# A feed-forward part cut into half-token units that begin inside the layer norm, with the normalising on ScalarE

## The chip, the cores and the metric

The kernel runs on one core of a Trainium2 chip. The core has a matrix engine (TensorE, PE in the profile, with its weight loads as PEld), three engines for elementwise work (VectorE = DVE, ScalarE = ACT, GpSimd = POOL), and a queue that issues transfers (SyncE = SP). The metric is the device time of one launch in microseconds, lower is better. All matmuls write PSUM, which has eight banks of 512 f32 values per partition; most other data lies in one large SBUF buffer called `arena`, of which the tiles named below are views.

## What is computed

One sequence of 1024 tokens and 512 features goes through four residual blocks, each followed by a layer norm without weights:

```python
x = _layernorm(x + _L0_attn_ref(x, ...))   # state-space scan, 16 states
x = _layernorm(x + _L0_ffn_ref(x, ...))    # silu(x Wg^T) * (x Wu^T), then Wd^T; inner width 1792
x = _layernorm(x + _L1_attn_ref(x, ...))   # causal attention, 32 heads of 16
x = _layernorm(x + _L1_ffn_ref(x, ...))    # the same with 4-bit weights, inner width 1376

def _layernorm(x, axis=-1, eps=1e-05):
    m = jnp.mean(x, axis=axis, keepdims=True)
    v = jnp.var(x, axis=axis, keepdims=True)
    return (x - m) / jnp.sqrt(v + eps)
```

The change is in the first layer norm and the first half (gate and up) of the first feed-forward block. It also touches one small step that all four layer norms share.

## The kernel before

Each engine runs its own instructions in the order in which they are written; semaphores join them. There is no scheduler: the order in the text is the order on the engine. Tokens come in 8 tiles of 128 (`TT = 8`, `P = 128`), the inner width in 14 tiles (`M0 = 14`), and the features in 4 chunks (`DC = 4`).

**After the scan.** The residual stream lies as `xT`, features on partitions. SP issues the load of the up weights (`wu0_sb`, line 404) and of the down weights (`wd0_sb`, line 406) when the scan's last product and last sum are done, both counted on `ld_w0`.

**The first layer norm** (`norm_stage(0)` on PE, ACT, DVE). For each token tile t, PE turns the tile to token-major with four transposes (`turn_residual`, line 619) into one bank of `LN_BANKS[0]` = 4, 5, 6, 7. DVE takes its statistics (`bn_stats`, line 1306; `bn_aggr`, line 1309), adds epsilon (line 1310, into `vare`), ACT takes the root (line 969), DVE the reciprocal (line 1314), and DVE writes the normalised tile `xn` (line 1324). PE turns it back (line 596) into bank 2 or 3, ACT copies it as f16 into `xh` (line 965, "high") and DVE writes the rest, again f16, into `xl` (line 1328, "rest"). POOL keeps `xn` in `xtok` for the next residual. DVE does a tile's steps one after the other, with the statistics of tile t+1 and the rest of tile t-1 between them. PE's order is: turn tile t, turn back tile t-2, and so on.

**Gate and up** (`gate_up0`, line 650). A unit is one tile of the inner width and all 1024 tokens: 32 matmuls of 128x512 f16, 16 for the gate (2 banks) and 16 for up (2 banks): 4 chunks, each for `xh` and `xl`, each for two halves of the tokens. The first unit's first half (16 matmuls, tokens 0 to 511) stands inside the norm, ahead of the last two tiles' turning back (`between=first_gate_up0`); it waits for four tiles of `xl` and, in `gate_up0`, for banks 4 to 7 to be read out. The other 432 matmuls follow when all eight tiles are there. ACT makes `sg` = silu(gate) (line 992, 1024 columns), DVE multiplies with up (line 1362), ACT copies the product as f16 (line 994, `hh`), DVE writes the rest (line 1364, `hl`). Two units are in flight. Behind each of the first four units ACT and DVE also split one of the attention's weight matrices (lines 986 and 1355).

**Down** (`down0`, line 674). For each token tile 28 matmuls over the 14 inner tiles. It starts when all silus and all but the last rest are done.

## Time and profile before

| | us |
|---|---|
| three runs, median (lowest to highest) | 921.18 (920.85 to 922.14) |
| the profiled execution, its own time | 922.86 |
| its span in the trace | 920.9 |
| first layer norm to the first gate and up matmul | 214.85 to 232.18 |
| the other 432 gate and up matmuls | 238.37 to 331.79 |
| share of the span in which PE is busy | 91% |

Times in the trace are counted from the start of the span; 1.96 us of the launch lie outside it. PE is busy 91% of the span, DVE 71%, ACT 44%, POOL 32%. The chain of work that ended last goes through PE for 69% of the span and through DVE for 14%.

### The profile page before, as it was taken

How to read it: one execution, taken by the hardware profiler on the slowest of the kernel's cores; microseconds unless marked ns; L12 is line 12 of the kernel's file. 1: busy time of each engine (PE TensorE's matmuls, PEld its weight loads, DVE VectorE, ACT ScalarE, POOL GpSimd, SP SyncE). 2: the span in 40 equal slices, each digit the busy share in tenths (PEclk: the TensorE clock that was granted, in tenths of full speed). 3: DMA queues.
4: the chain of work that ended last, by engine and by line, in shares of the span. 5: the costliest groups of instructions: out<-in, count | busy, mean ns of one | idle time of the engine just before them, and what ended most of it. 6: DMA issues, size and time to landing. Idle time of an engine off the chain costs nothing.

```text
span 920.9 us, 19770 instructions
## 1 busy us (share of the span) xinstructions
PE 835.9 (91%) x8209; PEld 396.4 (43%) x8209; DVE 654.1 (71%) x926; ACT 408.7 (44%) x478; POOL 297.4 (32%) x211
## 2 busy tenths in 40 slices
PE   7559797986999999999988999999987999999997
PEld 2325353544444444455533344344423444444443
DVE  4998999996563334545666989999965978886334
ACT  4525666642442321253443767776665343333100
POOL 0458999993010001164420221111223222222000
PEclk8679899996999999999977999999997999999999
DMA  7800000004420000000000000000013103430011
GB/s 230 321 1 3 3 3 3 3 3 160 134 66 0 0 1 1 0 1 1 1 1 1 2 2 2 2 1 2 2 53 116 56 6 144 129 111 0 1 46 46
DMA packets 21934, 38.21 MB, mean 41 GB/s; under 512 B 6993, under 2 KB 12881, under 8 KB 21858
## 3 DMA queue, kind: packets, MB, share of 16 engines
q1 hardware_dynamic: 21858, 37.11, 11.8%
q8 instruction: 59, 0.97, 0.4%
q14 instruction: 17, 0.14, 0.0%
HBM read 34.87 MB, written 2.16 MB: 40 GB/s over the span
## 4 chain that ended last, share of the span: by engine, by line
PE 69%; DVE 14%; issue 4%; ACT 3%; POOL 2%; SPq 1%; DMA 1%; DVEq 0%; POOLq 0%; ACTq 0%
PE ps L825 12%; PE ps L650 11%; PE ps L628 8%; PE ps L852 6%; PE ps L776 6%; DVE arena L1393 6%; PE ps L674 5%; PE ps L712 5%; PE ps L760 3%; POOL arena L1103 2%; PE ps L493 2%; DVE arena L1248 2%; PE ps L543 2%; PE ps L689 2%; PE ps L716 2%
## 5 line engine op out<-in xcount | busy, mean ns | idle before, releaser
L1393 DVE TENSOR_REDUCE arena<-ps 128x1 f32<-128x512 f32 (+3 forms) x320 | 183.6, 629 | 22.9 <-PE ps L716 15.9
L1050 ACT ACTIVATE arena<-ps 128x1024 f32<-128x1024 f32 (+2 forms) x160 | 144.2, 941 | 81.8 <-PE ps L760 81.6
L1103 POOL TENSOR_TENSOR arena<-arena 128x1024 f32<-128x1024 f32 x64 | 156.9, 2485 | 54.2 <-DVE arena L1248 52.6
L1248 DVE TENSOR_TENSOR_SCAN arena<-arena,ps 128x1024 f32<-128x1024 f32 x64 | 142.4, 2271 | 8.9 <-PE ps L543 6.7
L825 PE MATMUL ps<-arena 128*128 128x512 f16 x528 | 114.3, 379 | 1.6 <-DVE arena L1328 1.6
L1150 POOL TENSOR_SCALAR_AFFINE_SELECT arena<-arena 128x512 f32<-128x512 f32 x64 | 42.6, 667 | 189.4 <-ACT arena L1050 189.4
L712 PE MATMUL ps<-arena 64*128 64x512 f16 (+3 forms) x384 | 98.1, 344 | 1.0 <-DVE arena L1393 1.0
L944 ACT ACTIVATE arena<-arena,negA 128x1024 f32<-128x1024 f32 x64 | 72.6, 1147 | 58.9 <-DVE arena L1248 57.1
L650 PE MATMUL ps<-arena 128*128 128x512 f16 x448 | 97.2, 379 | 1.6 <-DVE arena L1328 1.6
L543 PE MATMUL ps<-arena 64*128 64x64 f16 x3072 | 61.2, 197 | 35.6 <-DVE arena L1248 28.5
L543 PEld LDWEIGHTS ps<-arena 64*128 64x128 f16 x3072 | 53.4, 99 | 86.1 <-DVE arena L1248 67.3
L628 PE MATMUL ps<-arena 128*128 128x512 f16 x384 | 86.9, 379 | 3.1 <-DVE arena L1328 1.6
L776 PE MATMUL ps<-arena 128*32 128x512 f32 (+3 forms) x768 | 84.8, 515 | 1.9 <-POOL arena L1150 1.9
L760 PE MATMUL ps<-arena 64*128 64x512 f16 (+3 forms) x384 | 77.9, 342 | 6.0 <-DMA arena<-arena 4.3
L825 PEld LDWEIGHTS ps<-arena 128*128 128x128 f16 x528 | 51.6, 98 | 63.6 <-DVE arena L1328 1.8
L493 PE MATMUL ps<-arena,ident_sb 64*64 64x512 f32 x512 | 73.9, 653 | 3.7 <-POOL arena L1103 3.6
L650 PEld LDWEIGHTS ps<-arena 128*128 (+1 forms) x448 | 43.9, 98 | 54.3 <-DVE arena L1328 1.8
L712 PEld LDWEIGHTS ps<-arena 64*128 64x128 f16 x384 | 29.3, 94 | 82.7 <-DVE arena L1393 70.1
L852 PE MATMUL ps<-arena 128*128 128x512 f16 x264 | 57.1, 379 | 0.0
L628 PEld LDWEIGHTS ps<-arena 128*128 128x128 f16 x384 | 36.3, 98 | 45.2 <-DVE arena L1302 1.9
L716 PE MATMUL ps<-mask_b,picks_b 64*128 64x128 bf16 x512 | 52.8, 221 | 0.0
L674 PE MATMUL ps<-arena 128*128 128x512 f16 x224 | 49.3, 379 | 0.0
(145 smaller groups left out, 976.7 us busy)
## 6 DMA issues: line engine op xcount, KB each, us to landing
arena<-in_w_q_dram SPq DMA_DIRECT2D x11, 768.0 KB, 4.2
arena<-c_rows SPq DMA_DIRECT2D x16, 512.0 KB, 10.9
arena<-in_w_s_dram SPq DMA_DIRECT2D x11, 384.0 KB, 4.6
arena<-in_x_fm_dram SPq DMA_DIRECT2D x8, 256.0 KB, 3.9
out_dram<-arena SPq DMA_DIRECT2D x8, 256.0 KB, 2.0
arena<-in_wg_dram SPq DMA_DIRECT2D x1, 1792.0 KB, 9.8
arena<-in_wu_dram SPq DMA_DIRECT2D x1, 1792.0 KB, 7.2
arena<-in_wd_dram SPq DMA_DIRECT2D x1, 1792.0 KB, 10.7
```

The lines of the kernel that those rows point to most:

```text
L543: last = nc.tensor.matmul(ps[:, 2 * (i % 2) + r, q * SUB:(q + 1) * SUB], dtx_tok[c % 2][rows, s, q, :], diag[n][rows, e, q, :], start=(k = ...
L628: last = nc.tensor.matmul(banks(bank, 1), part[:, c, ds(t * P, P)], wsp[:, w, s, c, :], start=(c == 0 and part is src_h and s == 0), stop= ...
L650: last = nc.tensor.matmul(banks(bank + h, 1), w[:, c, ds(m * P, P)], part[:, c, h * HALF:(h + 1) * HALF], start=(c == 0 and part is xh), s ...
L712: last = nc.tensor.matmul(dst, q_st[rows, 2 * g + r, i * P:(i + 1) * P], k_st[rows, 2 * g + r, key:key + w], start=True, stop=not diag)
L760: last = nc.tensor.matmul(ps[:, 3 + 2 * (e % 2) + b, at * (hi - lo):(at + 1) * (hi - lo)], k_st[rows, 2 * g + r, j * P:(j + 1) * P], q_st[ ...
L776: last = nc.tensor.matmul(ps[32 * a:32 * a + 32, 7, lo - HALF * half:HALF], v_ring[g % 2][:, j, a, :], p_t[n % 4][:, a, 0:hi - lo], start= ...
L825: last = nc.tensor.matmul(banks(bank + h, 1), gu[u][:, s, w * DC + c, :], part[:, c, h * HALF:(h + 1) * HALF], start=(c == 0 and s == 0 an ...
L852: last = nc.tensor.matmul(banks(u, 1), part[:, m, ds(t * P, P)], wd1[:, s, m, :], start=(m == 0 and part is h1h and s == 0), stop=(m == M1 ...
L1050: nc.scalar.activation(dst, src, ACT.Exp, scale=float(HD) ** -0.5).then_inc(exp_done, 1)
L1103: nc.gpsimd.tensor_tensor(hC[i % 4][:], hst[i % 3][:], c_all[:, n, :], ALU.mult).then_inc(hc_done, 1)
L1248: nc.vector.tensor_tensor_scan(hst[i % 3][:], dA[i % 3][:], banks(2 * (i % 2), 2), 0.0, ALU.mult, ALU.add).then_inc(scan_done, 1)
L1393: nc.vector.reduce_max(maxima_slot(half, k), ps[:, ring_bank(n), 0:len(heads) * w].rearrange("p (a w) -> p a w", a=len(heads)), AX).then_i ...
```

## The change

1. **Units.** A unit is now one inner tile and half the tokens: 16 matmuls, 8 for the gate in one bank and 8 for up in another. There are 28: the 14 tiles for tokens 0 to 511, then the 14 for tokens 512 to 1023. Up to four units are in flight (only two among the first four and the last four), so `sg` and `h32` have four slots of 512 columns. The loops are written out.
2. **Start.** PE turns the residual of tiles 0 to 3, turns back tiles 0 to 3 with tiles 4 and 5 of the residual between them, and then begins unit 0. The residual of tiles 6 and 7 and the turning back of tiles 4 to 7 stand between units 0 to 3. `LN_BANKS[0]` is now 0, 1, 4, 5, 0, 1, 0, 1.
3. **Normalising on ACT.** In the first norm, ACT writes `xn` as rstd * x + shift straight from PSUM; DVE makes `shift` = -mean * rstd, 128x1. The rest of DVE's steps stay.
4. **Epsilon.** In all four norms the root takes epsilon as its bias (`eps_sb`); DVE's addition into `vare` is gone. One small memset is added at the start of the program.
5. **Around it.** The down weights have their own semaphore `ld_wd0`, waited for at the first down matmul. The first four token tiles of down wait for the first 14 units' rests (and for 24 products, which frees banks 0 and 1), the later ones for all 28. The attention's weights are split behind units 6 to 9, each wait of theirs with them.

```diff
-LN_BANKS = ((4, 5, 6, 7), (0, 1), (0, 1), (0, 1))
+LN_BANKS = ((0, 1, 4, 5, 0, 1, 0, 1), (0, 1), (0, 1), (0, 1))
...
-        sg = view(104, 2 * T, f32).rearrange("p (b t) -> p b t", b=2)
-        h32 = view(112, 2 * T, f32).rearrange("p (b t) -> p b t", b=2)
+        sg = view(104, 4 * HALF, f32).rearrange("p (b t) -> p b t", b=4)
+        h32 = view(112, 4 * HALF, f32).rearrange("p (b t) -> p b t", b=4)
...
-        vare = small("vare", [P, 2])
+        eps_sb = small("eps_sb", [P, 1])
         sdev = small("sdev", [P, 2])
-        rstd = small("rstd", [P, 1])
+        rstd = small("rstd", [P, 2])
+        shift = small("shift", [P, 2])
...
+        UNITS0 = 2 * M0
+        def unit0_slot(n):
+            return n % 4 if 4 <= n < UNITS0 - 4 else n % 2
+        def unit0_before(n):
+            return next((o for o in range(n - 1, -1, -1) if unit0_slot(o) == unit0_slot(n)), None)
+        def unit_banks(slot):
+            return ((6, 7), (4, 5), (2, 3), (0, 1))[slot]
...
-            sp.dma_start(wd0_sb[:], wd0.rearrange("(m p) d -> p m d", p=P)).then_inc(ld_w0, 16)
+            sp.dma_start(wd0_sb[:], wd0.rearrange("(m p) d -> p m d", p=P)).then_inc(ld_wd0, 16)
...
-            def gate_up0(m, u, halves=(0, 1), first=False):
-                for w, bank, free, signal in ((wg0_sb, 4 - 4 * u, silu_done, gate_done), (wu0_sb, 6 - 4 * u, h_done, up_done)):
-                    if not first:
-                        pe.wait_ge(free, m - 1)
-                    elif halves == (0,):
-                        pe.wait_ge(x_normed, bank + 1)
+            def gate_up0(n):
+                h, m = divmod(n, M0)
+                gate, up = unit_banks(unit0_slot(n))
+                before = unit0_before(n)
+                for w, bank, free, signal in ((wg0_sb, gate, silu_done, gate_done), (wu0_sb, up, h_done, up_done)):
+                    if before is not None:
+                        pe.wait_ge(free, before + 1)
                     for c in range(DC):
                         for part in (xh, xl):
-                            for h in halves:
-                                last = nc.tensor.matmul(banks(bank + h, 1), w[:, c, ds(m * P, P)],
-                                                        part[:, c, h * HALF:(h + 1) * HALF],
-                                                        start=(c == 0 and part is xh), stop=(c == DC - 1 and part is xl))
-                    if halves != (0,):
-                        last.then_inc(signal, 1)
-            def first_gate_up0():
-                pe.wait_ge(ld_w0, 3 * 16)
-                pe.wait_ge(xl_done, TT // 2)
-                gate_up0(0, 0, (0,), first=True)
-            norm_stage(0, turn_residual, straight=True, between=first_gate_up0)
-            pe.wait_ge(xl_done, TT)
-            gate_up0(0, 0, (1,), first=True)
-            gate_up0(1, 1, first=True)
-            with pe.Fori(1, M0 // 2) as k:
-                for u in range(2):
-                    gate_up0(2 * k + u, u)
+                            last = nc.tensor.matmul(banks(bank, 1), w[:, c, m * P:(m + 1) * P], part[:, c, h * HALF:(h + 1) * HALF],
+                                                    start=(c == 0 and part is xh), stop=(c == DC - 1 and part is xl))
+                    last.then_inc(signal, 1)
+            def turn_first(t):
+                if t >= 4:
+                    pe.wait_ge(x_normed, (1, 2, 5, 6)[t - 4])
+                turn_residual(t, LN_BANKS[0][t]).then_inc(ln_in, 1)
+            def turn_normed(t):
+                pe.wait_ge(x_normed, t + 1)
+                if t >= 2:
+                    pe.wait_ge(xl_done, t - 1)
+                for c in range(DC):
+                    last = nc.tensor.transpose(ps[:, 2 + t % 2, c * P:(c + 1) * P], xn[:, t % 2, c * P:(c + 1) * P], ident_sb[:])
+                last.then_inc(x_turned, 1)
+            for t in range(4):
+                turn_first(t)
+            turn_normed(0)
+            turn_normed(1)
+            turn_first(4)
+            turn_normed(2)
+            turn_first(5)
+            turn_normed(3)
+            pe.wait_ge(ld_w0, 2 * 16)
+            pe.wait_ge(xl_done, TT // 2)
+            gate_up0(0)
+            turn_first(6)
+            turn_normed(4)
+            gate_up0(1)
+            turn_first(7)
+            turn_normed(5)
+            gate_up0(2)
+            turn_normed(6)
+            gate_up0(3)
+            turn_normed(7)
+            for n in range(4, UNITS0):
+                if n == 6:
+                    pe.wait_ge(xl_done, TT)
+                gate_up0(n)
             def down0(t, u):
                 for m in range(M0):
-                    if isinstance(t, int) and t == 0 and m == M0 - 1:
+                    if isinstance(t, int) and t == 0 and m == 0:
+                        pe.wait_ge(ld_wd0, 16)
                         pe.wait_ge(hl_done, M0)
+                        pe.wait_ge(h_done, UNITS0 - 4)
+                    if not (isinstance(t, int) and t < TT // 2) and m == 0:
+                        pe.wait_ge(hl_done, UNITS0)
                     for part in (hh, hl):
                         last = nc.tensor.matmul(banks(u, 1), part[:, m, ds(t * P, P)], wd0_sb[:, m, :],
                                                 start=(m == 0 and part is hh), stop=(m == M0 - 1 and part is hl))
                 return last
-            pe.wait_ge(silu_done, M0)
-            pe.wait_ge(hl_done, M0 - 1)
             norm_stage(1, down0, between=first_projections)
...
                 def root(t, u):
                     act.wait_ge(var_done, TT * ln + t + 1)
-                    nc.scalar.activation(sdev[:, u:u + 1], vare[:, u:u + 1], ACT.Sqrt).then_inc(sdev_done, 1)
+                    nc.scalar.activation(sdev[:, u:u + 1], mv[:, u, 1:2], ACT.Sqrt, bias=eps_sb[:]).then_inc(sdev_done, 1)
...
+            def first_normalise(t):
+                u = t % 2
+                act.wait_ge(shift_made, t + 1)
+                if t >= 2:
+                    act.wait_ge(x_kept, t - 1)
+                    act.wait_ge(x_turned, t - 1)
+                nc.scalar.activation(xn[:, u, :], banks(LN_BANKS[0][t], 1), ACT.Identity, bias=shift[:, u:u + 1],
+                                     scale=rstd[:, u:u + 1]).then_inc(x_normed, 1)
...
+            def gate_taken(n):
+                act.wait_ge(gate_done, n + 1)
+                if n >= 4:
+                    act.wait_ge(h_done, n - 3)
+                nc.scalar.activation(sg[:, n % 4, :], banks(unit_banks(unit0_slot(n))[0], 1), ACT.Silu).then_inc(silu_done, 1)
+            def product_high(n):
+                h, m = divmod(n, M0)
+                act.wait_ge(h_done, n + 1)
+                nc.scalar.copy(hh[:, m, h * HALF:(h + 1) * HALF], h32[:, n % 4, :]).then_inc(hh_done, 1)
+            first_root(0)
+            first_root(1)
+            first_normalise(0)
+            first_root(2)
+            first_normalise(1)
+            first_high(0)
+            first_root(3)
+            first_normalise(2)
+            first_high(1)
+            first_normalise(3)
+            first_high(2)
+            first_root(4)
+            first_high(3)
+            first_normalise(4)
+            first_root(5)
+            first_normalise(5)
+            for n in range(UNITS0):
+                gate_taken(n)
+                if n < 2:
+                    first_root(6 + n)
+                    first_normalise(6 + n)
+                if n < 4:
+                    first_high(4 + n)
+                product_high(n)
+                if 6 <= n < 10:
+                    weight_high(n - 6)
...
                 def variance(t, u):
-                    own.done(nc.vector.bn_aggr(mv[:, u, :], st6[:]))
-                    nc.vector.tensor_scalar(vare[:, u:u + 1], mv[:, u, 1:2], EPS, None, ALU.add).then_inc(var_done, 1)
+                    nc.vector.bn_aggr(mv[:, u, :], st6[:]).then_inc(var_done, 1)
+                    dve.wait_ge(var_done, TT * ln + t + 1)
                 def root_taken(t, u):
                     dve.wait_ge(sdev_done, TT * ln + t + 1)
-                    own.done(nc.vector.reciprocal(rstd[:], sdev[:, u:u + 1]))
+                    own.done(nc.vector.reciprocal(rstd[:, 0:1], sdev[:, u:u + 1]))
...
+            def first_stats(t):
+                dve.wait_ge(ln_in, t + 1)
+                own.done(nc.vector.bn_stats(st6[:], banks(LN_BANKS[0][t], 1)))
+                if t >= 2:
+                    dve.wait_ge(sdev_done, t - 1)
+                nc.vector.bn_aggr(mv[:, t % 2, :], st6[:]).then_inc(var_done, 1)
+                dve.wait_ge(var_done, t + 1)
+            def first_shift(t):
+                u = t % 2
+                dve.wait_ge(sdev_done, t + 1)
+                if t >= 2:
+                    dve.wait_ge(x_normed, t - 1)
+                own.done(nc.vector.reciprocal(rstd[:, u:u + 1], sdev[:, u:u + 1]))
+                nc.vector.scalar_tensor_tensor(shift[:, u:u + 1], mv[:, u, 0:1], -1.0, rstd[:, u:u + 1], ALU.mult, ALU.mult).then_inc(shift_made, 1)
+            def first_rest(t):
+                dve.wait_ge(xh_done, t + 1)
+                nc.vector.tensor_tensor(xl[:, :, t * P:(t + 1) * P], ps[:, 2 + t % 2, :].rearrange("p (c t) -> p c t", c=DC),
+                                        xh[:, :, t * P:(t + 1) * P], ALU.subtract).then_inc(xl_done, 1)
...
+            def product(n):
+                dve.wait_ge(silu_done, n + 1)
+                dve.wait_ge(up_done, n + 1)
+                if n >= 4:
+                    dve.wait_ge(hl_done, n - 3)
+                nc.vector.tensor_tensor(h32[:, n % 4, :], sg[:, n % 4, :], banks(unit_banks(unit0_slot(n))[1], 1), ALU.mult).then_inc(h_done, 1)
+            def product_rest(n):
+                h, m = divmod(n, M0)
+                dve.wait_ge(hh_done, n + 1)
+                at = slice(h * HALF, (h + 1) * HALF)
+                nc.vector.tensor_tensor(hl[:, m, at], h32[:, n % 4, :], hh[:, m, at], ALU.subtract).then_inc(hl_done, 1)
...
+            first_stats(0)
+            first_stats(1)
+            first_shift(0)
+            first_stats(2)
+            first_shift(1)
+            first_stats(3)
+            first_shift(2)
+            first_rest(0)
+            first_shift(3)
+            first_rest(1)
+            first_stats(4)
+            first_rest(2)
+            first_rest(3)
+            first_shift(4)
+            first_stats(5)
+            first_shift(5)
+            for n in range(UNITS0):
+                product(n)
+                if n < 2:
+                    first_stats(6 + n)
+                    first_shift(6 + n)
+                if n < 4:
+                    first_rest(4 + n)
+                product_rest(n)
+                if 6 <= n < 10:
+                    weight_low(n - 6)
...
```

On PE, from the end of the scan, the order before is this (L619 turns the residual, L596 turns back, L650 is gate and up):

```order
L619 MATMUL ps<-ident_sb,arena 128x128 x12
L596 MATMUL ps<-ident_sb,arena 128x128 x4
L619 MATMUL ps<-ident_sb,arena 128x128 x4
L596 MATMUL ps<-ident_sb,arena 128x128 x4
L619 MATMUL ps<-ident_sb,arena 128x128 x4
L596 MATMUL ps<-ident_sb,arena 128x128 x4
L619 MATMUL ps<-ident_sb,arena 128x128 x4
L596 MATMUL ps<-ident_sb,arena 128x128 x4
L619 MATMUL ps<-ident_sb,arena 128x128 x4
L596 MATMUL ps<-ident_sb,arena 128x128 x4
L619 MATMUL ps<-ident_sb,arena 128x128 x4
L596 MATMUL ps<-ident_sb,arena 128x128 x4
```

Then come 16 matmuls of L650, 8 of L596, and the rest of L650. After the change PE has, from the first turning back on (L632 turns the residual, L678 turns back, L664 is gate and up):

```order
L678 MATMUL ps<-ident_sb,arena 128x128 x8
L632 MATMUL ps<-ident_sb,arena 128x128 x4
L678 MATMUL ps<-ident_sb,arena 128x128 x4
L632 MATMUL ps<-ident_sb,arena 128x128 x4
L678 MATMUL ps<-ident_sb,arena 128x128 x4
L664 MATMUL ps<-arena 128x512 x16
L632 MATMUL ps<-ident_sb,arena 128x128 x4
L678 MATMUL ps<-ident_sb,arena 128x128 x4
L664 MATMUL ps<-arena 128x512 x16
L632 MATMUL ps<-ident_sb,arena 128x128 x4
L678 MATMUL ps<-ident_sb,arena 128x128 x4
L664 MATMUL ps<-arena 128x512 x16
```

The first 16 matmuls of gate and up have moved from behind the turning of all eight residual tiles and six of the tiles back to behind six and four; six groups of transposes that stood ahead of or beside them now stand between units.

On ACT, from the end of the norm's first part, the order after the change is this (L1023 root, L1031 normalising, L1036 high, L1047 silu, L1052 copy of the product); before, all roots and highs were done ahead of the first silu, with one table load between them:

```order
L1031 ACTIVATE arena<-ps,shift,rstd 128x512
L1047 ACT_TABLE_LOAD
L1047 ACTIVATE arena<-ps 128x512
L1023 ACT_TABLE_LOAD
L1023 ACTIVATE sdev<-mv,eps_sb 128x1
L1031 ACTIVATE arena<-ps,shift,rstd 128x512
L1036 CAST arena<-ps 128x4x128
L1052 CAST arena<-arena 128x512
L1047 ACT_TABLE_LOAD
L1047 ACTIVATE arena<-ps 128x512
L1023 ACT_TABLE_LOAD
```

The roots of tiles 6 and 7 have moved in between the silus of units 0, 1 and 2, and each change from the one function to the other and back loads a table: five loads up to the silu of unit 2 where there was one.

## Rows read from the trace of the kernel before

**Rows 1.** Windows: PE, PEld, DVE, ACT, POOL busy (instructions), granted clock, DMA.
```profile
214.85:232.50 17.65, 12.64 (x57) 10.38 (x58) 15.80 (x40) 5.08 (x13) 3.69 (x6) 0.60 0.58 183
232.50:238.40 5.90, 4.34 (x25) 2.34 (x24) 3.95 (x9) 2.72 (x5) 1.23 (x2) 1.00 0.91 346
238.40:331.80 93.40, 93.40 (x433) 42.35 (x434) 40.97 (x30) 35.10 (x32) 3.75 (x2) 1.00 0.10 27
```

**Rows 2.** The chain that ended last around the first norm: start, length, what.
```profile
215.98 0.71 DVE st L1306
...
231.27 1.11 PE ps L596 x4
232.38 3.55 PE ps L650 x16
...
236.41 0.59 ACT arena L965
237.03 1.30 DVE arena L1328 x2
```

**Rows 3.** The same chain further on, its long pieces.
```profile
238.37 93.41 PE ps L650 x432
331.79 18.13 PE ps L674 x84
...
728.26 0.44 PE ps L596 x4
728.70 2.59 PE ps L628 x12
```

**Rows 4.** Timeline of one token tile in the first norm: start, length, engine, line.
```profile
226.64 0.69 DVE L1306 BATCH_NORM_STATS2 st<-ps 128x6 f32<-128x512 f32 x1
...
227.36 0.16 DVE L1314 RECIPROCAL rstd<-sdev 128x1 f32<-128x1 f32 x1
227.43 0.59 ACT L965 CAST arena<-ps 128x512 f32 x1 [1.80 <-PE ps L596]
227.56 0.18 DVE L1309 BATCH_NORM_AGGREGATE mv<-st 128x2 f32<-128x6 f32 x1
227.78 0.15 DVE L1310 TENSOR_SCALAR vare<-mv 128x1 f32<-128x1 f32 x1
227.86 0.81 DVE L1324 TENSOR_SCALAR arena<-ps,mv,rstd 128x512 f32<-128x512 f32 x1
227.96 0.20 ACT L969 ACTIVATE sdev<-vare 128x1 f32<-128x1 f32 x1
228.59 0.68 DVE L1328 TENSOR_TENSOR arena<-ps,arena 128x512 f16<-128x512 f32 x1
```

**Rows 5.** Timeline of ACT near the start, without and with a 128x1 operand.
```profile
18.70 0.70 ACT L880 ACTIVATE arena<-arena,series_sb 128x512 f16<-128x512 f32 x1
19.32 0.61 ACT L881 ACTIVATE arena<-arena 128x512 f32<-128x512 f32 x1
```

**Rows 6.** Timeline of ACT between the last root and the first silu.
```profile
237.50 1.28 ACT L992 ACT_TABLE_LOAD   x1
```

**Rows 7.** Windows of the norm, columns as in rows 1, for the granted clock.
```profile
212.00:222.00 10.00, 6.99 (x33) 5.00 (x26) 7.13 (x17) 3.53 (x7) 1.23 (x2) 0.50 0.96 323
222.50:225.50 3.00, 1.25 (x10) 0.86 (x8) 2.86 (x9) 1.21 (x4) 0.62 (x1) 1.00 0.31 97
226.00:232.00 6.00, 4.67 (x20) 3.87 (x21) 5.79 (x15) 1.48 (x4) 1.85 (x3) 0.50 0.18 7
```

**Rows 8.** Timeline of PE's transposes at the higher clock, and of SP's load.
```profile
211.57 0.38 SPq L404 DMA_DIRECT2D arena<-in_wu_dram  x1
...
223.64 0.65 PE L596 MATMUL ps<-ident_sb,arena 128*128 128x128 f32 x4 [0.98 <-DVE arena L1324]
```

**Rows 9.** The page's DMA issues: KB each, us from issue to landing.
```profile
arena<-in_wu_dram SPq DMA_DIRECT2D x1, 1792.0 KB, 7.2
```

48 lines of the change are left out of this document (13 added, 35 removed).

## The prediction

> **What bounds the kernel now.** I read the windows by stage first, then the chain of waits, then the timeline of one tile. The windows show three stretches around the change [rows 1]. In the first, 214.85 to 232.5 us, DVE is busy for 15.80 of 17.65 us, while PE has only transposes: the first layer norm is bound by DVE. In the third, 238.4 to 331.8 us, PE is busy all the time at the full granted clock: gate and up are bound by PE. The second is the seam: 16 gate and up matmuls are run early, and then PE stands for 1.5 us at the end of the norm. The chain of waits says the same [rows 2]. It goes from the first statistics at 215.98 through DVE, tile by tile, up to the transposes at 231.27, the 16 early matmuls at 232.38, the copy and the two rests at 236.41 and 237.03, and then without a break through 432 matmuls [rows 3]. These take 93.41 us, 0.2162 us each, so all 448 need 96.9 us of PE. They cover 214.85 to 331.79, 116.9 us. So 20.0 us of PE's time around the norm hold no gate and up work. This is what the change can win from. A token tile costs DVE 0.69 + 0.16 + 0.18 + 0.15 + 0.81 + 0.68 us, 2.67, and with small overlaps about 2.55; the rest of tile 3, the last of these rows, ends at 229.27 [rows 4].
>
> **Part 1, normalising on ACT.** DVE loses the 0.81 us and the addition of 0.15, and gains `shift`, a 128x1 step that I price like the addition, 0.15 [rows 4]. That leaves DVE 1.9 us a tile. ACT gains the normalising. No row shows it. An ACT instruction on 128x512 out of PSUM takes 0.59 [rows 4], and a 128x1 operand adds about 0.1 (0.70 against 0.61) [rows 5]. The new one has two such operands, so I take 0.82, with bounds 0.59 (they cost nothing beyond) and 0.94. By the same row the root with its bias goes from 0.20 to 0.30. ACT then has 0.30 + 0.82 + 0.59 = 1.7 us a tile and was idle most of the time there (5.08 of 17.65 busy) [rows 1].
>
> **Part 2, when unit 0 can begin.** I walk the engines' new orders by hand with these durations and 0.04 us for each hand-over. The first statistics stay at 215.98. The first normalising starts at 218.2; tiles 0 to 3 are normed by 219.0, 220.3, 222.0 and 223.4. ACT is the tight engine here: from 218.2 it has four normalisings, four highs and three roots, 6.5 us, and with its short waits ends the fourth high at 225.1. DVE then writes the fourth rest by 225.8, where it was 229.3 before. Unit 0 begins at 225.9 instead of the 232.2 of the 16 early matmuls. The weights are no obstacle: the up weights are issued at 211.57 [rows 8] and take 7.2 us to landing [rows 9], so they are there by 218.8; the down weights, issued behind them, are now waited for only at the first down matmul, 100 us later.
>
> **Part 3, from there PE's queue alone.** Behind 225.9 PE has 448 matmuls, 96.9 us, and six groups of four transposes, 0.44 us each at the full clock [rows 3]: 2.6 us. That would end gate and up at 325.4. That one unit writes eight matmuls in a row into one bank adds nothing: in the attention's projections twelve in a row into one bank take 2.59 us, 0.216 each [rows 3]. The copies of weights behind units 6 to 9 keep their cost; each unit leaves ACT and DVE about 2 us free, and with up to four units in flight the walk shows no wait of PE.
>
> **Part 4, the loop through the tables.** The new order puts the roots of tiles 6 and 7 between the silus, and only two units may be in flight until unit 4. From silu 0 to silu 1, and again to silu 2, ACT has: silu 0.59, load of the root's table 1.28, a wait of 0.3 for the statistics, root 0.30, 0.4 for DVE's reciprocal and shift, normalising 0.82, high 0.59, product's copy 0.59, load of the silu's table 1.28. That is 6.2 us a round [rows 4, 6]. Silu 0 can start at 229.8 (the table is loaded by then), so silu 2 ends at 242.9. PE reaches unit 4, which needs that silu's bank, 16.5 us after 225.9, at 242.4. PE so waits 0.5 us; the cover is used up, and every further microsecond on this loop would be paid in full. The end of gate and up goes to 325.9.
>
> Here a rule of the Trainium skill speaks against the change. The row shows that a table load takes 1.28 us [rows 6]. The page "ScalarE: Activation LUTs", section "Table sets: the hidden batching unit", says to batch calls by set and not by function, and gives about 2.7 us for a load. By the page's figure the walk ends gate and up at about 332.4 us, no better than now; the trace's duration is used, so the sum keeps 325.9.
>
> **Part 5, the clock.** PE's granted clock was at the lower of its two levels, 1.2 GHz, in 212 to 222, with transposes for 6.99 of 10 us. It was at 2.4 GHz in 222.5 to 225.5, where PE was busy for only 1.25 of 3 us; it then fell again, and stayed low from 226 to 232 with 4.67 of 6 us busy [rows 7]. From 232.5 on it is full [rows 1]. In my walk PE has three groups of transposes between 222 and 225.9 and waits for the rest of it, as sparse as the stretch before the fall. So I expect the first matmuls at the lower level. The bounds are none of it, and the whole low stretch with PE at work nearby, which by these rows is 6 to 7 us long; I take the middle, 3.4 us, which costs half of that, 1.7 us. It gives ACT time, so the 0.5 us of part 4 vanishes. Sum: 325.4 + 1.7 = 327.1, against 331.79: **4.7 us** sooner.
>
> **Part 6, what follows.** Down starts with its first four token tiles, which need units 0 to 13 alone, and banks 0 and 1, free after unit 23; both are past by then, so PE runs on as it does at 331.79 now [rows 3]. The later tiles need the last rest, which comes about 2.5 us after the last unit, against 24 us of down. The addition of epsilon is gone in 24 more tiles, but in the second norm PE sets the pace (28 matmuls a tile), and in the third too: 0.44 + 2.59 = 3.03 us is the whole period of a tile [rows 3]. Only the starts and the end of the norms are on the path, 0.04 to 0.07 each, less than what the bias adds to the root. I take -0.1, with bounds -0.3 and +0.3. The memset at the start lies beside the loads. Written-out loops add no work; one row of 432 matmuls shows no gap for the loop that there was, so nothing is gained either.
>
> **The sum.** -4.7 - 0.1 = -4.8 us. The profiled execution took 922.86 us, 1.68 more than the median of the three runs; on its own scale the forecast is 918.1. Taken to the median, 921.18 - 4.8 = **916.4 us**.
>
> **Rivals.**
> 1. *Full clock from the start.* The transposes now come more densely, and the clock stays up. End of gate and up 325.9, so 915.2; with a normalising of 0.59 us the walk gives 325.0 and 914.2. For it: the loss of part 5 is read from one fall only. Against: that fall came after just such a sparse stretch.
> 2. *The four tiles come no sooner.* If ACT's chain in the norm is as long as DVE's was (tile 3 ready at 229.3), then only PE's order gains: 229.3 + 96.9 + 2.6 = 328.8, -3.0, and up to 1.7 of clock on top: 918.2 to 919.9, about 918.8. Against: the tile's work is now split 1.9 to 1.7 between two engines, where 2.55 stood on one.
> 3. *The table loop binds* (no change). It decides when a round costs ACT more than 6 us; at 7.5 us a round, by longer loads, or waits where I have hand-overs, unit 4 comes about 3 to 5 us later and the time is 919.5 to 921.5, about 920.5. For it: slack is nil. Against: the row of 1.28.
> 4. *Slower: low clock through the mixed stretch.* The clock counts on a busy PE; if waits of units 1 to 4 on the table loop keep it at 1.2 GHz, 64 matmuls and 24 transposes take 33 us instead of 16.5. That costs 16.5 against the 6.4 us of room: 921.18 + 10 = 931. It decides at 12.8 us of low clock. Against: PE has long, unbroken stretches of 3.5 us there, and the rise by 232.5 came after less.
>
> **How the numbers follow.** The forecast has 0.62, rival 1 0.15, rival 2 0.12, rival 3 0.07, rival 4 0.04. The forecast's own bounds: clock 0 to 3.4, stall 0 to 1, normalising, later norms; 914.7 to 918.5. The range takes in rivals 1 and 2, 914.0 to 919.2, and leaves out rivals 3 and 4. About 0.2% (1.8 us) can be told from no change. Faster by more than that: the forecast, rivals 1 and most of 2, 0.88; within it: rest of 2 and rival 3, 0.08; slower 0.04.
>
> **What would show it.** The first gate and up matmul near 225.9 (rival 2: 229.3). A few matmuls of 0.43 us pitch, then 0.216. The last one at about 327.1, and no idle PE before the first down matmul. Normalising near 0.8 us on ACT. Five table loads of 1.28 before the silu of unit 2, and a wait of PE ahead of unit 4 of 0 to 0.5 us (rival 3: several). The forecast would be wrong if the fourth rest came after 227, if PE waited for silus in more than one place, or if another stage, above all the attention, changed its length.

## The result: 913.8 us, 7.1 us faster, 2.3 us more than forecast

| | before | changed |
|---|---|---|
| median of the runs measured side by side (lowest to highest), us | 920.85 (918.77 to 922.14) | 913.77 (911.17 to 915.73) |
| ratio, with its 95% interval | | 0.9921 [0.9903, 0.9939] |
| the profiled execution, its own time and its span, us | 922.86, 920.9 | 914.36, 912.6 |
| from the first transpose of the norm to the last gate and up matmul ("the seam"), us | 116.5 | 110.7 |
| attention: first key product to first gate and up product of the last block, us | 263.5 | 258.9 |

The forecast was 916.4 us with a range of 914.0 to 919.2. The time is just below the range, and the sign is right. The changed kernel measured again gave 0.9906 [0.9887, 0.9925] and 913.72 us.

The windows by stage are those of [rows 1] and [rows 7] (columns as there: PE, PEld, DVE, ACT, POOL busy, granted clock, DMA):

```profile
212.00:222.00 10.00, 6.40 (x35) 4.27 (x36) 4.82 (x12) 4.11 (x7) 2.86 (x3) 0.71 0.64 220
222.00:226.50 4.50, 3.99 (x20) 3.55 (x19) 3.87 (x11) 3.97 (x7) 1.97 (x4) 0.50 1.03 325
226.50:228.59 2.09, 0.59 (x7) 0.39 (x6) 1.62 (x5) 0.88 (x2) 0.05 (x1) 1.00 0.00 0
228.59:245.10 16.51, 16.51 (x88) 8.95 (x88) 7.43 (x19) 14.18 (x20) 2.47 (x4) 1.00 0.39 128
245.10:327.90 82.80, 82.78 (x385) 37.50 (x385) 43.89 (x56) 37.51 (x57) 3.75 (x2) 1.00 0.11 31
```

Between 228.59 and 245.10, where units and tiles are mixed, PE is busy all the time and ACT for 14.18 of 16.51 us. The hole of 1.5 us behind the early matmuls, seen in the second window of [rows 1], is gone. One of 1.5 us now stands ahead of unit 0, where PE waits for the high copy and the rest of tile 3 (227.13 and 227.75 in the chain below). The chain that ended last shows the same, and is to be read against [rows 2] and [rows 3] (L1433 statistics, L1031 normalising, L632 and L678 transposes, L1036 high, L1449 rest, L664 gate and up, L715 down):

```profile
218.30 0.71 DVE st L1433
...
222.22 0.79 ACT arena L1031
...
223.05 1.12 PE ps L678 x4
224.16 0.85 PE ps L632 x4
225.02 0.85 PE ps L678 x4
225.87 0.79 PE ps L632 x4
226.66 0.45 PE ps L678 x4
...
227.13 0.60 ACT arena L1036
...
227.75 0.70 DVE arena L1449
...
228.59 3.61 PE ps L664 x16
232.20 0.44 PE ps L632 x4
232.64 0.44 PE ps L678 x4
233.07 3.45 PE ps L664 x16
...
251.84 76.41 PE ps L664 x354
328.25 11.87 PE ps L715 x55
```

This execution lost 2.3 us before the norm: its first statistics are at 218.30, where [rows 2] have 215.98. In it the input projection's last matmul starts at 17.0 us, in the kernel before at 14.0; in the other profile of the changed kernel it is 14.2. So the stage is measured from its own start. Difference of the spans, 8.3 us: start -2.3 (a loss), seam +5.8, attention +4.6, the rest 0.2. For the pair of profiles taken later (c1 and c2 below, 918.5 and 911.2): start -0.9, seam +6.2, attention +1.9, the rest 0.1. In these two pairs the seam is steady. The attention differs as well, by an amount that varies, though the change touches in it nothing but epsilon.

The down weights' own semaphore did no work in these profiles: in the changed kernel both loads have landed before unit 0 starts (up 221.85, down 227.01, unit 0 228.59; in its second profile down 224.02, unit 0 226.89).

### The profile page after: what moved, and what is told of

Same layout as the page of the kernel before. It is cut to its first block, busy times and chain, and to the rows that moved or that the text cites. A ratio compares the mean times of both kernels' runs of the same rounds, so it can differ in the third digit from the quotient of the medians.

```text
span 912.6 us, 19633 instructions
## 1 busy us (share of the span) xinstructions
PE 831.6 (91%) x8209; PEld 394.4 (43%) x8209; DVE 650.5 (71%) x923; ACT 427.2 (47%) x518; POOL 297.2 (33%) x211
## 4 chain that ended last, share of the span: by engine, by line
PE 68%; DVE 13%; issue 4%; ACT 3%; POOL 3%; DMA 1%; SPq 1%; POOLq 0%; DVEq 0%; ACTq 0%
PE ps L864 13%; PE ps L664 11%; PE ps L641 8%; PE ps L891 6%; DVE arena L1518 6%; PE ps L815 5%; PE ps L715 5%; PE ps L751 4%; PE ps L799 3%; POOL arena L1182 3%; PE ps L506 2%; DVE arena L1328 2%; PE ps L556 2%; PE ps L728 2%; PE ps L755 1%
## 5 line engine op out<-in xcount | busy, mean ns | idle before, releaser
L664 PE MATMUL ps<-arena 128*128 128x512 f16 x448 | 97.5, 379 | 1.5 <-DVE arena L1449 1.5
L864 PEld LDWEIGHTS ps<-arena 128*128 128x128 f16 x528 | 51.6, 98 | 63.6 <-DVE arena L1408 1.8
L664 PEld LDWEIGHTS ps<-arena 128*128 128x128 f16 x448 | 43.7, 98 | 53.7 <-issue 1.7
L641 PEld LDWEIGHTS ps<-arena 128*128 128x128 f16 x384 | 36.4, 98 | 45.0 <-DVE arena L1382 1.8
L715 PE MATMUL ps<-arena 128*128 128x512 f16 x224 | 49.3, 379 | 0.0
## 6 DMA issues: line engine op xcount, KB each, us to landing
arena<-in_wd_dram SPq DMA_DIRECT2D x1, 1792.0 KB, 11.4
```

The lines of the kernel that those rows point to most:

```text
L641: last = nc.tensor.matmul(banks(bank, 1), part[:, c, ds(t * P, P)], wsp[:, w, s, c, :], start=(c == 0 and part is src_h and s == 0), stop= ...
L664: last = nc.tensor.matmul(banks(bank, 1), w[:, c, m * P:(m + 1) * P], part[:, c, h * HALF:(h + 1) * HALF], start=(c == 0 and part is xh), ...
L864: last = nc.tensor.matmul(banks(bank + h, 1), gu[u][:, s, w * DC + c, :], part[:, c, h * HALF:(h + 1) * HALF], start=(c == 0 and s == 0 an ...
```

## Experiments

In each table row "seam" and "attention" are as above. "first unit" is the time from the norm's first transpose to the first gate and up matmul; "matmuls" is from there to the last one's start. Ratio and median come from 4 to 12 executions of each kernel. The other four columns come from one profiled execution each, and are differences of times read to 0.1 us, so they can be off by 0.1.

| | ratio to before | median us | first unit | matmuls | seam | attention |
|---|---|---|---|---|---|---|
| before | | 920.85 | 17.3 | 99.2 | 116.5 | 263.5 |
| c1 before, again | 0.9996 [0.9982, 1.0009] | 920.92 | 16.6 | 100.5 | 117.1 | 261.2 |
| changed | 0.9921 [0.9903, 0.9939] | 913.77 | 11.4 | 99.3 | 110.7 | 258.9 |
| c2 changed, again | 0.9906 [0.9887, 0.9925] | 913.72 | 11.7 | 99.2 | 110.9 | 259.3 |
| e1 epsilon only | 0.9989 [0.9974, 1.0004] | 919.95 | 16.9 | 99.6 | 116.5 | 259.8 |
| e2 ACT normalises, old order | 1.0038 [1.0024, 1.0053] | 924.84 | 19.7 | 100.1 | 119.8 | 261.1 |
| e3 the same, ACT's queue reordered | 1.0017 [0.9997, 1.0037] | 923.49 | 17.1 | 100.6 | 117.7 | 261.2 |
| e4 new order, DVE normalises | 0.9948 [0.9933, 0.9964] | 916.89 | 12.8 | 101.2 | 114.0 | 259.1 |
| e5 new units, no early start | 1.001 [0.9998, 1.0021] | 923.15 | 20.6 | 99.3 | 119.9 | 259.1 |
| e6 changed, addition of epsilon back | 0.9915 [0.9903, 0.9928] | 913.91 | 11.4 | 100.8 | 112.2 | 258.1 |
| e7 before, 58 more PE instructions | 1.0002 [0.9986, 1.0017] | 920.32 | 16.4 | 99.4 | 115.8 | 261.1 |
| e8 changed, 82 more | 0.9892 [0.9874, 0.9909] | 911.66 | 11.5 | 99.3 | 110.8 | 257.3 |
| e9 changed, table loads doubled | 0.9996 [0.9984, 1.0008] | 920.41 | 11.7 | 106.1 | 117.8 | 259.6 |
| e10 before, 116 more | 0.9973 [0.9962, 0.9985] | 918.92 | 17.2 | 100.5 | 117.7 | 261.3 |
| e11 changed, 123 more | 0.9894 [0.9879, 0.9908] | 912.75 | 11.2 | 99.2 | 110.4 | 256.2 |
| e12 changed, 166 more | 0.9917 [0.9899, 0.9935] | 914.17 | 11.4 | 100.8 | 112.2 | 260.7 |
| e13 before, 207 more | 0.9983 [0.9971, 0.9995] | 919.90 | 17.3 | 100.8 | 118.1 | 257.6 |

**The two kernels again** (c1, c2), for how much one profile tells.

> The kernel before, unchanged, as a control. Theory A (the change acts only between the first transposes of the norm and the last gate and up matmul; the other differences between the two profiles are scatter of single executions): ratio 1.000 +- 0.002, but stretches outside the seam move between profiles of the same kernel by as much as they did between before and after: the start up to the last x_proj matmul (14.0 us before, 17.0 after) and the first attention steps (477.1 to 499.8 before, 473.6 to 494.0 after) by 2 to 4 us. Theory B (the change itself shortens the attention by 3.9 us): the attention stretch repeats within 0.5 us of the first profile of before.

> The changed kernel, unchanged. Theory A: ratio near 0.993, first norm transpose to last gate and up matmul again 110.7 us (before 116.5), if the granted clock is again full when unit 0 begins; 112.4 if it is at the lower level for 3.4 us. The attention stretch 473.6 to 692.9 (219.3 us; before 223.1) changes by 2 us or more. Theory B: it stays within 0.5 us of 219.3.

The seam repeats within 0.6 us. The attention of the kernel before does not: it differs by 2.3 us between two executions of one kernel, that of the changed kernel by 0.4. One profile of each kernel therefore tells little of the attention.

### The parts of the change

**e1, epsilon alone.** The kernel before, with this in all four norms:

```diff
-                    nc.scalar.activation(sdev[:, u:u + 1], vare[:, u:u + 1], ACT.Sqrt).then_inc(sdev_done, 1)
+                    nc.scalar.activation(sdev[:, u:u + 1], mv[:, u, 1:2], ACT.Sqrt, bias=eps_sb[:]).then_inc(sdev_done, 1)
```

> The kernel before with epsilon as the root's bias in all four norms, nothing else. My forecast had -0.1 us (bounds -0.3 to +0.3) for the three later norms. In the first norm DVE loses one 128x1 step a tile that mostly overlapped (0.08 each): -0.6 us. Together -0.7, ratio 0.9992. Rival: epsilon carries more of the gain, since what lies behind the seam moved by 2.4 us in the profiles (3.5 ahead after gate and up, 8.2 at the end, less 3.0 late at the start): -2 us or more, ratio 0.998 or less.

0.9989, with 1 inside the interval; the seam is unchanged at 116.5. **e6** asks the same from the other side: the changed kernel with DVE's addition in the last three norms.

```diff
-                    nc.vector.bn_aggr(mv[:, u, :], st6[:]).then_inc(var_done, 1)
-                    dve.wait_ge(var_done, TT * ln + t + 1)
+                    own.done(nc.vector.bn_aggr(mv[:, u, :], st6[:]))
+                    nc.vector.tensor_scalar(vare[:, u:u + 1], mv[:, u, 1:2], EPS, None, ALU.add).then_inc(var_done, 1)
```

> The changed kernel with the addition of epsilon on VectorE restored in norms two to four. By my walk +0.1 to +0.3 us. The changed kernel gains 7.1 to 7.8 us in all, and only 5.8 to 6.0 of it lie in the seam. Theory A (the rest is scatter): ratio to before as that of the changed kernel, 0.990 to 0.993. Rival (epsilon makes the rest): +1.5 us, ratio 0.993 to 0.994, and the stretches behind the seam that differ would come back.

0.9915 against 0.9921 and 0.9906: epsilon is worth nothing that can be told, and the attention's gain is not epsilon's (e6 does without that part of the change and has 258.1).

**e2 and e3, the normalising alone.** e1, and in the first norm ACT normalises; PE's order and the units are those of before. In e2 ACT's queue has a tile's copy `high` behind the next tile's normalising:

```diff
+                    for t in range(2, TT):
+                        root(t, t % 2)
+                        act_norm(t - 1, (t - 1) % 2)
+                        high(t - 2, t % 2)
```

> The kernel before with epsilon as bias and the first norm's normalising on ScalarE, but with the old order on PE and the old units of 1024 tokens. Eight tiles by 1.9 us of DVE instead of 2.55: the last rest comes some 4 to 5 us sooner, if PE's old order does not bind; PE's 16 early matmuls then start at about 228 instead of 232. My theory: -3.5 to -4.5 us against before, that is the larger part of the gain is the split of the tile between the two engines. Rival: ACT's chain binds as DVE's did (rival 2 of the prediction): -1 us or less.

It is slower by 0.4%, where 3.5 to 4.5 us less were expected. The chain of e2, one tile's round (L1373 and L1376 statistics, L1385 shift, L976 normalising, L966 high):

```profile
222.21 0.70 DVE st L1373
...
222.93 0.19 DVE mv L1376
...
223.34 0.17 DVE shift L1385
...
223.54 0.78 ACT arena L976
...
224.32 0.48 ACT arena L966
...
225.43 0.70 DVE st L1373
```

DVE waits for `high` before its rest, `high` stands behind the normalising, that waits for DVE's shift, and the next statistics stand behind the rest: 3.2 us a tile, where DVE alone took 2.55 [rows 4]. In e3 `high` stands ahead of the normalising:

```diff
-                        act_norm(t - 1, (t - 1) % 2)
                         high(t - 2, t % 2)
+                        act_norm(t - 1, (t - 1) % 2)
```

> As the run with the old PE order and old units and the normalising on ScalarE, but on ScalarE each tile's high copy stands ahead of the next tile's normalising, where that run had it behind. In its trace the steps stats, shift, normalising, high, rest of neighbouring tiles formed one serial loop of 3.2 us a tile (before: 2.55). Theory A (that loop was an artefact of my order): now DVE binds at 1.9 us a tile, first transposes to last gate and up matmul 112 to 114 us (before 116.5), time -3 to -4.5 us. Rival (moving the normalising to ScalarE costs more in hand-overs than it relieves DVE, whatever the order): 116 us or more, no gain.

2.47 us a tile, by the spacing of the statistics in its chain, and the time of before (1.0017, with 1 inside the interval); 1.9 us a tile had been expected. So moving 0.81 us from the bounding engine to a mostly idle one gained nothing by itself: the tile's steps still went through both engines one after the other.

**e4, the order alone.** The changed kernel, with DVE normalising in one step again; ACT's normalising is left out:

```diff
-                nc.vector.scalar_tensor_tensor(shift[:, u:u + 1], mv[:, u, 0:1], -1.0, rstd[:, u:u + 1], ALU.mult, ALU.mult).then_inc(shift_made, 1)
...
+                nc.vector.tensor_scalar(xn[:, u, :], banks(LN_BANKS[0][t], 1), mv[:, u, 0:1], rstd[:, u:u + 1],
+                                        ALU.subtract, ALU.mult).then_inc(x_normed, 1)
```

> The changed kernel with the first norm's normalising back on VectorE, order and units as changed. DVE then has, up to the fourth rest, five statistics of 0.9, four reciprocals of 0.2, four normalisings of 0.81 and four rests of 0.69: 11.3 us from the first statistics, so unit 0 begins 12.4 us after the first transpose (changed kernel 11.4 to 11.7). Theory A (the early start carries the gain): 1 us slower than the changed kernel, ratio to before 0.992 to 0.994. Rival (the split of the tile carries it): 3 us slower or more, ratio 0.995 or above.

The first unit comes 1.1 to 1.4 us later than with ACT, and the seam is 114.0: 3.2 us longer than in the changed kernel, still 2.5 to 3 shorter than before. The other 2 us are clock in this profile. Two windows of e4:

```profile
222.00:228.20 6.20, 3.50 (x17) 2.73 (x15) 5.47 (x12) 2.23 (x5) 1.36 (x3) 0.51 0.45 141
228.20:236.00 7.80, 7.75 (x31) 3.69 (x32) 4.11 (x9) 3.91 (x6) 1.23 (x2) 0.73 0.01 2
```

The transposes ran at the lower level to the end and the first matmuls began there. That DVE's normalising brought this lower level is not shown: e6 and e12 below pay 1.6 us of the same kind with ACT normalising. By the ratios e4 (0.9948) is 2.5 to 3.9 us slower than the changed kernel (0.9921, 0.9906); its interval overlaps that of the first result and lies clear of those of c2 and e6. So the early start carries more than half of the gain. The two recorded theories had 0.992 to 0.994 and 0.995 or above, and the result stands between them.

**e5, the units without the early start.** The changed kernel; all eight tiles are normed first (the same lines move ahead in ACT's and DVE's queues, so no table is exchanged between the first units):

```diff
-            pe.wait_ge(xl_done, TT // 2)
-            gate_up0(0)
...
             turn_normed(7)
-            for n in range(4, UNITS0):
+            pe.wait_ge(xl_done, TT)
+            for n in range(UNITS0):
```

> The changed kernel, but unit 0 begins only when all eight tiles are normed; no table swap in between. Eight tiles at 1.9 us from the first statistics end about 16.5 us after the first transpose, then 96.9 us without a break: 113.5 us to the last matmul, against 110.7 with the early start and 116.5 before. Time 2.8 us above the changed kernel. Rival: the interleaving costs as much as it gains (swaps, clock), then within 1 us of the changed kernel.

The first unit starts 20.6 us after the first transpose, where 16.5 were expected, and the gain is gone (1.001). Part of this is my order of the last tiles, in which tiles 5 to 7 again went through ACT and DVE one at a time. Another part is the clock: the granted clock is 0.50 from 236.02 to 241.60, the first 5.6 us of matmuls, and by the table the matmuls then take 99.3 us where 447 times 0.216 are 96.6: a cost of some 2.7 us, by this estimate. So the seam of 119.9 is longer than it need be, and what the units gain without the early start is not measured cleanly. What e5 does show is that this kernel without its early start gains nothing; and that, with the seam lost, its attention was still at 259.1.

### The loop through the tables

**e9.** The changed kernel, and in each of the two rounds a silu and a root of one column on ACT, which bring two more table loads:

```diff
                     first_root(6 + n)
+                    nc.scalar.activation(spare[:, 2 * n:2 * n + 1], eps_sb[:], ACT.Silu)
+                    nc.scalar.activation(spare[:, 2 * n + 1:2 * n + 2], eps_sb[:], ACT.Sqrt)
                     first_normalise(6 + n)
```

> The changed kernel with two more table loads and two 1-column activations in each of the two rounds between silu 0 and silu 2 (the root's and the silu's table alternately). My walk had the loop at 6.2 us a round and no slack: the end of gate and up would come 2 x 2.7 = 5.2 us later, first transposes to last gate and up matmul 116 us, time 5 us above the changed kernel. Rival (the loop has slack, since PE's own work up to unit 4 is as long): 1 to 3 us. If the price of a load were the page's 2.7 us and not 1.28, twice that.

Two groups of lines from the timelines: first the changed kernel's second round (ACT, and PE's unit 4), then e9's second round.

```profile
238.49 0.60 ACT L1047 ACTIVATE arena<-ps 128x512 f32<-128x512 f32 x1
239.11 1.28 ACT L1023 ACT_TABLE_LOAD   x1
...
240.67 0.30 ACT L1023 ACTIVATE sdev<-mv,eps_sb 128x1 f32<-128x1 f32 x1 [0.28 <-DVE mv L1436]
...
241.45 0.78 ACT L1031 ACTIVATE arena<-ps,shift,rstd 128x512 f32<-128x512 f32 x1 [0.48 <-DVE shift L1445]
...
243.25 1.28 ACT L1047 ACT_TABLE_LOAD   x1
...
244.54 0.60 ACT L1047 ACTIVATE arena<-ps 128x512 f32<-128x512 f32 x1
...
245.20 1.04 PE L664 MATMUL ps<-arena 128*128 128x512 f16 x4
```

```profile
239.30 1.28 ACT L1024 ACT_TABLE_LOAD   x1
...
241.18 1.28 ACT L1075 ACT_TABLE_LOAD   x1
...
242.68 1.28 ACT L1076 ACT_TABLE_LOAD   x1
...
245.86 1.28 ACT L1048 ACT_TABLE_LOAD   x1
246.19 1.09 PE L679 MATMUL ps<-ident_sb,arena 128*128 128x128 f32 x4 [3.22 <-DVE arena L1452]
247.15 0.60 ACT L1048 ACTIVATE arena<-ps 128x512 f32<-128x512 f32 x1
...
247.80 4.58 PE L665 MATMUL ps<-arena 128*128 128x512 f16 x11 [0.52 <-ACT arena L1048]
```

In the changed kernel a round takes 6.05 us from silu to silu; the third silu ends at 245.14, and unit 4, which needs its bank, starts at 245.20. It is exactly in time. In e9 a round takes 8.46 us, 2.41 more, for two loads of 1.28 and two small steps of 0.20, less a wait for DVE of 0.48 that they cover and small overlaps. PE stands 3.2 and 0.5 us; its transposes then take 1.09 us, where the same view has 0.60 elsewhere, which is the lower clock level, and the 11 matmuls 0.42 each. The two rounds are 4.8 us longer and the seam 6.9, so the whole gain of the kernel is lost. What the loop gains in length is paid in full, and the clock on top.

### What the attention gave

Without added waits (all but e7, e8 and e10 to e13), the kernels with the new units had an attention of 258.1 to 259.6 us, those with the old ones 259.8 to 263.5. A place in the chain where they differ is the last of its 16 groups of four small row transfers. First the kernel before (c1 reads the same, 2.41 at the end), then c2, the changed kernel again:

```profile
683.25 0.59 SPq L426
683.88 2.49 DMA arena<-arena
```

```profile
676.23 0.59 SPq L439
...
676.87 1.70 DMA arena<-arena
```

The view of transfers in the 4 us around this group (682 to 686) shows for the kernel before one more packet, which is not data:

```profile
q8 instruction: 1, 0.02, 1.6%
arena<-arena SPq DMA_DIRECT2D x4, 1.0 KB, 2.3
```

and for c2 none in 3.6 us, with

```profile
arena<-arena SPq DMA_DIRECT2D x4, 1.0 KB, 1.7
```

Such a packet brings 16 KB of instructions. By their places they are PE's: in the attention they come about every 250 records of PE and PEld. So their place depends on the length of PE's program ahead of them. The written-out loops changed that length. In all 17 profiles, each group of row transfers that took 3.7 us or more from its first issue to its last landing, where others take 3.5 to 3.6, had such a packet within that time; not each group with a packet was late.

The experiments add redundant waits of PE late in the scan, where all it waits for is long there; two of them share one instruction, and an odd one has one of its own. For e7, the kernel before:

```diff
+                    if 31 <= i < 60:
+                        for _ in range(4):
+                            pe.wait_ge(warm_set, 1)
```

> The kernel before with 116 redundant waits added on TensorE (four ahead of each of 29 steps at the end of the scan, on a semaphore that has long its value); nothing else. In the five profiles with the old units a 16384-byte instruction packet lies over two of the attention's small row transfers, which then land in 2.2 to 3.1 us; in the five with the new, written-out units it lies elsewhere and they land in 1.6 to 1.7. Theory L (layout: TensorE's longer program shifts the places where its instructions are fetched): the pads shift them as the new units do, the second and the last group of row transfers land in 1.7, keys first to last 219.5 us instead of 221, and the time is 1.5 to 2.5 us below before, less what the waits cost in the scan (0 to 1.5). Rival: the transfers are slower for another reason; landing stays at 2.2 to 3.1, no gain.

> The changed kernel with 140 redundant waits on TensorE (five ahead of each of 28 steps at the end of the scan). Theory L: with 116 places of the shift taken up to a full 256, the instruction packet lies over the two groups of row transfers again: landing 2.2 to 3.1 us, keys first to last about 221, the time 1.5 to 2.5 us above the changed kernel, ratio to before about 0.994, plus what the waits cost (0 to 1.8). Rival: landings stay at 1.7, the time moves only by the waits.

e7's 116 waits became only 58 instructions (19828 instructions in the profile, 19770 before), so the packet moved half as far as meant, still within the last group, and the time stayed. e8 (140 waits, 82 instructions) was expected to be slower than the changed kernel. It moved other groups into and out of reach and has the lowest median of the study, 911.66 us, with an interval that overlaps that of the changed kernel. e10 (8 waits in place of 4) and e11 (9 in each of 25 steps) followed:

> The kernel before, computing all, with 232 redundant waits of TensorE in the late steps of the scan. The 116 waits of the last such run became 58 instructions, two waits to one, so these should be 116 more instructions, about what the changed kernel has more of (its instruction packet lies 129 records further from the end). Theory (place of TensorE's instruction packets against the small row transfers of the attention): the last and the second of the sixteen groups of row transfers, which took 4.1 to 4.8 us to land in the kernel before, take 3.5 as in the changed kernel; the attention from its first key product to its last matmul gets 1.0 to 2.5 us shorter (before 223.1 and 220.5 us), less what the extra waits cost in the scan (under 0.5 us), median 919 to 920.5 against 921. Rival (the attention's gain has another cause in the changed kernel, such as the state of its queues or of the clock): the pattern of the groups may move, the attention keeps 220.5 to 223 us and the time is the same or 0.3 us more.

> The changed kernel, computing all, with 225 redundant waits of TensorE in the late steps of the scan, some 125 instructions more: with the 129 that it already has it comes to about 256, one whole instruction packet, so the packets should lie against the row transfers as in the kernel before. Theory (place of the packets): the second, fourth and last groups of row transfers take 4.1 to 4.8 us again, the attention takes 220.5 to 223 us instead of 219.3 to 219.8, and the time is 915 to 916.3 instead of 913.75, so that the gain left is that of the seam, 5 to 6 us. Rival (another cause): attention and time as in the changed kernel, 913.5 to 914.2.

In e10 the packet left the last group; its chain there ends with

```profile
683.69 0.59 SPq L426
684.33 1.69 DMA arena<-arena
```

and its 160 exponentials keep c2's distance from the first one within 0.1 us up to the 32nd and 0.8 us to the end. The time is 2.5 us better than before (0.9973), by redundant instructions alone. Its profile, a slow one for its kernel (921.63 us, median 918.92), does not show that gain in the attention, 261.3 us: it avoids c1's 2.3 us in the last group, but loses 2.4 us that c1 does not lose, 1.2 of them in the first groups. e11, expected at 915 to 916.3 us, went past the place I aimed at: the packets were still some 20 to 50 records from those of the kernel before, no group from the tenth on was late, the attention was the shortest of all, 256.2 us, and the median 912.75. So I aimed twice more, e12 (11 waits in each of 28 steps) at the place of before in the changed kernel, e13 (15 in each of 26) at e11's place in the kernel before:

> The changed kernel, computing all, with 308 redundant waits of TensorE in the late steps of the scan, two to an instruction: 168 more instructions. With 125 more (the run before this one) its instruction packets still lay 31 to 54 records from those of the kernel before, and no group of row transfers from the tenth to the sixteenth waited for one; 168 should bring them to within some 10 records of the kernel before. Theory (place of the packets): the second, fourth, seventh to ninth, fourteenth and last groups take 4.1 us and more as in the kernel before and the thirteenth 3.5; the attention from its first key product to the first gate or up product of the second feed-forward part takes 260.5 to 263 us (before 261.2 and 263.5, changed kernel 258.9 and 259.3, with 125 more 256.2); the ratio to the kernel before is 0.992 to 0.996, 2 to 4 us above the kernel with 125 more (0.9894). Rival (the written-out units help the attention in another way): attention 256 to 259.5 us, ratio 0.989 to 0.992.

> The kernel before, computing all, with 390 redundant waits of TensorE in the late steps of the scan, two to an instruction: 208 more instructions. That should bring its instruction packets to where they lay in the changed kernel with 125 more. Theory: the groups of row transfers from the tenth on take 3.5 us, the attention takes 256 to 258.5 us instead of 261.2 and 263.5, the scan may pay up to 1 us for the waits; ratio 0.994 to 0.997. Rival (only the written-out units gain there): attention 260 to 262 us, ratio 0.9995 to 1.002.

The last group in e12's chain, then in e13's:

```profile
677.47 1.63 SPq L439
679.14 0.59 SPq L439
679.77 1.70 DMA arena<-arena
```

```profile
682.92 0.59 SPq L426
683.55 1.70 DMA arena<-arena
```

The row transfers came out near what was aimed at in e12, less so in e13, where the eleventh and the fourteenth group are late (4.1 us each). In e12 one issue takes 1.63 us, the second, fourth, seventh, eighth, fourteenth and last groups are late again (and the twelfth, which was not late before; the ninth is on time), and the attention takes 260.7. In e13 it takes 257.6, 3.6 less than c1. Yet in the times little of this arrives: e12 with 0.9917 is between the two results of the changed kernel, and e13 with 0.9983 gained 1.6 us. In e13's profile 3.6 us were lost ahead of the attention (first transpose at 215.6 for c1's 214.3, seam 118.1, and from the seam to the attention 146.9 instead of 145.6 us), so that its span is c1's, 918.5.

What follows. **Shown** is that a packet beside a group of row transfers makes them late, and that redundant PE instructions alone can lower the time of the kernel before: 0.9973 [0.9962, 0.9985] in e10, against 1.0002 [0.9986, 1.0017] in e7. In the changed kernel the same kind of edit gave 0.9892 to 0.9917, which is not clear of noise (e8, e11 and e12 have intervals that overlap). Within one kernel the attention moved by 3.7 to 4.5 us with the added instructions (257.6 to 261.3 before, 256.2 to 260.7 changed), more than the 2.3 us between two profiles of one and the same kernel, but each of these is one profile.

**Not shown** is that this is why the changed kernel's attention is shorter. With like places it remains shorter, e12 against c1 by 0.5 us, c2 against e10 by 2.0, e11 against e13 by 1.4; all three are below those 2.3 us. Over four places each, the mean ratio is 0.9904 for the changed kernel (0.9914, 0.9892, 0.9894, 0.9917) and 0.9989 for the one before (0.9996, 1.0002, 0.9973, 0.9983): 7.8 us apart, of which the seam is 6. The cause of the last 1 to 2 us stays open.

One thing goes along with the attention's length over the 17 profiles, and that is how long the granted clock was at the lower level in it: 31.8 us of the 263.5 before, 29.8 of 261.2 in c1, 23.1 of 259.3 in c2, 22.5 of 258.9 in the changed kernel's first profile, 18.5 of 257.6 in e13 and 17.4 of 256.2 in e11. Over the 17 a microsecond more at the lower level goes with 0.43 us more of attention. Before, c1, e2, e3 and e7 have a spell of it that begins 206 to 209 us after the first key product, right behind the late last group; none of the kernels in which that group is on time has one there. The late transfers may so cost more through the clock than by their own delay. Which is cause and which effect these runs do not tell, and e1 and e12 have a late last group without the spell.

## The prediction, point by point

**What bounds it: right.** The 20 us around the norm without gate and up work were where most of the gain was; 448 matmuls and six groups of transposes from 228.59 to 328.25 take 99.7 us, forecast 96.9 + 2.6.

**Part 1, right.** The normalising took 0.78 us for 0.82, the root 0.30 as forecast. `shift` took 0.16 us at most tiles, but 0.55 to 0.58 at two where it ran beside other work. What the prediction did not see is that part 1 brings nothing without part 2 (e2, e3); with it, it is worth 1.1 to 1.4 us of the start, and 2.5 to 3.9 us in all by e4's ratio.

**Part 2, right in kind.** Unit 0 was forecast 9.9 us behind the first statistics and came 10.3 behind (228.59 - 218.30). Rival 2, the four tiles no sooner, is out.

**Part 3, right.** 3.45 us for 16 matmuls (0.216 each), 0.44 for a group of transposes.

**Part 4, right to some tenths of a microsecond.** Before the silu of unit 2 there were five loads of 1.28 us; a round took 6.05 us for 6.2, with no slack and no stall. "Every further microsecond on this loop would be paid in full" is what e9 shows, 6.9 us for 4.8. Rival 3 lies one table load away. The Trainium skill's page "ScalarE: Activation LUTs", section "Table sets: the hidden batching unit", gives about 2.7 us a load, by which the gain was nil; the rows of 1.28 decided, and e9 shows what longer loads would have done. Its advice to batch by set is to be weighed by slack: four extra loads cost nothing here, eight cost all.

**Part 5, the step that failed in the seam: the 1.7 us.** It was to come from the lower clock in the first 3.4 us of matmuls. In the changed kernel's two profiles it was 0: in the second window above, the transposes run at 0.50 with PE busy 3.99 of 4.50 us, and the clock rises at 226.5, ahead of unit 0. I had expected it high at 222 with a sparse PE behind it. The low clock made the transposes slow enough to stand back to back (chain above, 223.05 to 226.66), where PE in [rows 7] had pauses. That they do so does not decide it alone: in e12 the same five groups stand back to back at the lower level, from 220.61 to 225.1, and the clock rose only at 230.1. (The Trainium skill's page "TensorE: Matmul & The Clock Gate", section "Part 4: PE-mode transpose", says that transposes do not count as a busy TensorE in the same way. Here the clock rose at 226.5 with nothing but f32 transposes on PE since 217.17, so for these the trace does not bear it out.) But the price was not wrong, only its chance. In e12 (and e6 alike) the clock was high before 219.8 and fell for the transposes; e12's window and its first matmuls:

```profile
226.60:234.00 7.40, 7.37 (x31) 3.54 (x32) 2.79 (x9) 5.30 (x7) 1.23 (x2) 0.77 0.01 2
```

```profile
226.63 5.30 PE ps L667 x16
```

5.30 us for 16 matmuls instead of 3.61 is 1.7 us, the number forecast, and e12 and e6 have seams of 112.2. Of the six profiles whose first norm and loop are those of the change (changed, c2, e6, e8, e11, e12), four paid nothing and two paid 1.6. That is a mean of 0.5, where I put 1.7. What decides between the two stays open. Rival 1, full clock, is closer to what came; I gave it 0.15 for having read one fall in one profile.

**Part 6, the second step that failed: nothing for the attention.** I took 0.1 us for all that follows, and named a change of the attention's length as what would upset the forecast. It gave 1.9 us in one pair of profiles and 4.6 in the other. The argument for the norms holds (e1, e6). What it left out is that a change of code length ahead of a stage can itself act on that stage (e10); whether it did so here is open.

**The sum.** Forecast -4.8, measured -7.1 on the median. The seam gave 5.8 to 6.2 in place of 4.7: +1.7 for the clock, about -0.5 for unit 0. The remaining 1 to 2 us lie in the attention, cause open. The clock alone would not have left the range: with it at nothing, the walk gives 915.2 (rival 1). What carried the time past 914.0 is the attention's part, and 0.3 us by which the median of before was lower side by side (920.85) than the 921.18 that the forecast was taken from. The range was too tight because it held nothing for either direction outside the seam; two profiles of the same kernel before already differ by 2.4 us in span.
